# A pre-LN retention and mixture-of-experts layer on eight cores: smaller staging buffers, evacuation moved to VectorE, one copy of the odd heads, one wait ahead of the down projection

## The chip, the cores and the metric

One Trainium2 chip, all 8 of its cores. Each core takes one sequence of the batch (4096 tokens of 1024 features) and computes the whole layer for it; nothing is exchanged between cores. The metric is the device time of the slowest core, in microseconds (us), over one execution.

## The reference, cut to what matters

```python
x = x + attn(layernorm(x))      # retention: 16 heads of 64
x = x + ffn(layernorm(x))       # 8 experts and a shared one

# attn: Q, K, V = x @ Wq, Wk, Wv
scores = Q K^T * Dm / 8         # Dm: per head g**(i-j), lower triangle
out    = scores @ V             # no softmax
c      = groupnorm(out)         # one mean and variance per head over all 4096 tokens
return (c * gn_weight + gn_bias) @ Wout

# ffn: every expert on every token (g, u: 1024 -> 1408; w_down: 1408 -> 1024)
eo  = (silu(x @ w_gate[e]) * (x @ w_up[e])) @ w_down[e]
out = sum_e combine[e] * eo[e] + sigmoid(x @ shared_gate) * shared(x)
```

`combine` holds the renormalised softmax weights of the two best experts and zeros for the others, so all nine feed-forward blocks (eight experts and the shared one) run over all tokens.

## The kernel before, in words

Five instruction streams (TensorE, VectorE, ScalarE, SyncE, GpSimd) are written out by hand. `em(engine, fn)` appends to a stream and semaphores tie the streams together; each stream runs strictly in the order written. There are three blocks with a barrier of all engines between them.

**Block 0** (lines 212 to 242) loads the masks and the four attention matrices (cast to bf16 by the GpSimd queue's DMAs).

**Phase 1** (lines 312 to 622) runs over 8 chunks of 512 tokens. Per chunk, in order: ScalarE computes layer norm 1 (`emit_ln_sc`, line 123) from `x_sb`; TensorE transposes the result (`emit_t512a`); TensorE makes 24 groups of 8 matmuls, 8 each for q, k and v (`tqkv`, line 346), through two PSUM banks; each group is evacuated to bf16, q by VectorE (`vqkv`) and k and v by ScalarE (`sqkv`). The odd heads lie on partitions 64 to 127 and must be copied to partitions 0 to 63. SyncE does that in eight steps (`qk2`, line 402): for each `et` it waits for q and k of that `et`, issues one DMA of 64 KB from `qt_sb` and one from `kt_sb`, and waits until both have landed before the next step. Then come 16 steps of attention (`t_p1`, `v_1`, `s_ku`, `t_p2`, `v_2`, `s_tb`), of which the first, line 435 to 437, waits for all evacuations and all copies. At the end SyncE stores the chunk's output (`spill`), and VectorE and ScalarE gather the group norm's sums (`vstat`, `sstat`).

SyncE's order in a chunk is: load of the next chunk's x (`ldx`, after layer norm 1), wait for it, `qk2`, `spill`.

Alongside, GpSimd converts the expert weights to bf16: 27 pieces (nine blocks of gate, up, down), each 5.5 MB of f32 read from HBM into `stg` (2.75 MB as bf16) and then written back to `wbf`. One `stg` exists, so read and write alternate, each waiting for the one before to land (`emit_conversions`, line 284). Nothing ties these pieces to the chunks.

**Phase 2** (lines 777 to 1077) runs over 8 tiles of 512 tokens. Per tile: transposes with group norm folded in (`emit_t512b`), output projection (`twout`, line 835) and residual (`vwout`, line 848), layer norm 2, transposes, router, and then nine experts. For an expert TensorE makes 11 gate/up groups (16 matmuls each, lines 971 and 975). After each, ScalarE applies silu (line 987) and copies u (line 988), and VectorE multiplies them into `h_sb` (line 997). Then TensorE makes 8 down groups of 11 matmuls (`tdown`, line 1033), each evacuated by VectorE with a multiply-add into `x1` (line 1049). The first of the 8 groups (`didx == 0`) waits for the eleven blocks of h one at a time, just before the matmul that reads each:

```python
for it in range(NIT):
    if didx == 0:
        t.wait_ge(S("vch").h, htg[it])
    ins = t.matmul(db, ...)
```

The weights pass through `wring`, a ring of three slots of 2816 KB. The slots of gate and up come free together when ScalarE has copied the last u of the expert, so the loads for the next expert's gate and up (line 738, GpSimd's queue) start there and run beside the 88 down matmuls. The slot of down comes free after the last down group.

`x_sb` is one buffer of 4 x 1024 f32 per partition. In phase 2 the next tile's x is loaded into it after the output projection has read it (`ldx2`, line 860).

Of the kernel before, what the change touches and what calls it, by code (L numbers as in the profile page):

```python
# [10 lines left out]
F32 = mybir.dt.float32  # L11
# [6 lines left out]
C = 128  # L18
SC = 512
# [42 lines left out]
def build_nc(dbg=False, phases=(1, 2), nsc=None, p1_att=True, p1_qkv=True, p1_gn=True, p1_stats=True,  # L62
# [17 lines left out]
    dmask_h = nc.dram_tensor("dmask", [C, NH * C], F32, kind="ExternalInput").ap()  # L80
# [18 lines left out]
    x_sb = sb("x_sb", [C, 4 * D], F32)  # L99
    cols = sb("cols", [C, 32], F32)  # L100
    sqdump = sb("sqdump", [C, 2 * D], BF16)
# [3 lines left out]
    bcast = sb("bcast", [C, 32], F32)  # L105
# [17 lines left out]
    def emit_ln_sc(src, dst, per_tt_wait=None):  # L123
        ss = S("sc1")

        def s_ln(sc):
            for tt in range(4):
                if per_tt_wait is not None:
                    w = per_tt_wait[tt]
                    sc.wait_ge(S(w[0]).h, w[1])  # L130
                if tt >= 2:
                    sc.drain()
                sc.activation(sqdump[:, (tt % 2) * D:(tt % 2 + 1) * D],  # L133
                              src[:, tt * D:(tt + 1) * D], AF.Identity,
                              accum_out=cols[:, tt:tt + 1])
                sc.drain()
                sc.activation(sqdump[:, (tt % 2) * D:(tt % 2 + 1) * D],
                              src[:, tt * D:(tt + 1) * D], AF.Square,
                              accum_out=cols[:, 4 + tt:5 + tt])
# [33 lines left out]
    with contextlib.ExitStack() as p1es:  # L173
# [3 lines left out]
        dmask = sb1("dmask_sb", [C, NH * C], F32)  # L177
# [18 lines left out]
        stg = sb1("stg", [C, WSLOT], BF16)  # L196
# [87 lines left out]
        def emit_conversions(n):  # L284
            def gconv(g, plist=tuple(range(conv_state["p"], min(conv_state["p"] + n, PPT)))):
                for p in plist:
                    if p >= 1:
                        g.wait_ge(S("gcs0").h, 16 * p)
                    g.dma_start(out=stg[:, :], in_=conv_src(p)).then_inc(S("gcv0").h, 16)
                    g.wait_ge(S("gcv0").h, 16 * (p + 1))  # L290
                    g.dma_start(out=wbf_h[p], in_=stg[:, :]).then_inc(S("gcs0").h, 16)
            for p in range(conv_state["p"], min(conv_state["p"] + n, PPT)):
                S("gcv0").n += 16
                S("gcs0").n += 16
            conv_state["p"] = min(conv_state["p"] + n, PPT)
            em("gpsimd", gconv)
# [15 lines left out]
        for c in range(nsc):  # L312
# [30 lines left out]
            for gidx, (kind, idx) in enumerate(groups):  # L343
# [28 lines left out]
                if kind == "q":  # L372
                    def vqkv(v, idx=idx, bk=bk, tgt=S("peq").n):
                        v.wait_ge(S("peq").h, tgt)
                        ins = v.tensor_copy(qt_sb[:, idx * SC:(idx + 1) * SC], bk)
                        ins.then_inc(S("vcq").h, 1)
                    S("vcq").n += 1
                    evac_tgts.append(("vcq", S("vcq").n))
                    q_evac[idx] = ("vcq", S("vcq").n)
                    em("vector", vqkv)  # L380
                else:
                    def sqkv(sc, kind=kind, idx=idx, bk=bk, tgt=S("peq").n):
                        sc.wait_ge(S("peq").h, tgt)
                        if kind == "k":
                            dst = kt_sb[:, idx * SC:(idx + 1) * SC]
                        else:
                            tt, ec = idx // 2, idx % 2
                            dst = v_sb[:, tt * D + ec * 512:tt * D + (ec + 1) * 512]
                        ins = sc.copy(dst, bk)
                        ins.then_inc(S("scq").h, 1)  # L390
                    S("scq").n += 1
                    evac_tgts.append(("scq", S("scq").n))
                    if kind == "k":
                        k_evac[idx] = ("scq", S("scq").n)
                    em("scalar", sqkv)
            qkv_done_v = S("vcq").n
            qkv_done_s = S("scq").n

            for et in range(8):
                S("sld").n += 32  # L400
# [10 lines left out]
                em("sync", qk2)  # L411
# [11 lines left out]
            def emit_p1(m):  # L423
# [6 lines left out]
                def t_p1(t, ccx=ccx, heads=heads, a_bank=a_bank, ktr0=ktr0, m=m,  # L430
                         qtgt=qkv_done_v, stgt=qkv_done_s, q2tgt=qk2_done,
                         atgt=att_done_prev, vtgt=(vca_v1.get(m - 2, 0)),
                         kutgt=scku_m.get(m - 2, 0)):
                    if m < 2:
                        t.wait_ge(S("vcq").h, qtgt)
                        t.wait_ge(S("scq").h, stgt)
# [164 lines left out]
            def sstat(sc, tgt=att_done):  # L601
# [3 lines left out]
                for h in range(NH):  # L605
                    if h >= 2:
                        sc.drain()
                    ins = sc.activation(sqdump[:, (h % 2) * 256:(h % 2) * 256 + 256],
                                        src3[:, :, h * HE:(h + 1) * HE],
# [78 lines left out]
    with contextlib.ExitStack() as p2es:  # L688
# [87 lines left out]

        for t_i in range(NTILE):
            x1 = x1_sb[:, (t_i % 2) * 4 * D:(t_i % 2 + 1) * 4 * D]

            if t_i == 0:  # L780
                S("sld").n += 128

                def ld0(s, tgt=S("sld").n):
                    for tt in range(4):
                        s.dma_start(out=combt_sb[:, tt * D:(tt + 1) * D],
                                    in_=comb_h[tt * C:(tt + 1) * C, :]).then_inc(S("sld").h, 16)
                        ins = s.dma_start(out=x_sb[:, tt * D:(tt + 1) * D],
# [32 lines left out]
            for tloc in range(4):  # L820
                for dc in range(2):
# [21 lines left out]
                    def vwout(v, tloc=tloc, dc=dc, bk=bk, tgt=S("pew").n, x1=x1,  # L843
                              sttgt=(store_tgts[t_i - 2] if (gidx == 0 and t_i >= 2) else None)):
# [3 lines left out]
                        ins = v.tensor_add(x1[:, tloc * D + dc * 512:tloc * D + (dc + 1) * 512],  # L848
                                           x_sb[:, tloc * D + dc * 512:tloc * D + (dc + 1) * 512],
# [6 lines left out]

            if t_i + 1 < NTILE:
                S("sld").n += 64

                def ldx2(s, t_n=t_i + 1, wtgt=wout_done, tgt=S("sld").n):  # L860
                    s.wait_ge(S("vcw").h, wtgt)
                    for tt in range(4):
                        ins = s.dma_start(out=x_sb[:, tt * D:(tt + 1) * D],
# [88 lines left out]
            for e in range(NEXP):  # L952
                p0 = PPT * t_i + 3 * e
                hb = (e % 2) * NIT * SC
                h_tgts = {}
                for it in range(NIT):
# [45 lines left out]
                    h_tgts[it] = S("vch").n  # L1002
# [8 lines left out]
                for tloc in range(4):  # L1011
                    for dc in range(2):
# [4 lines left out]
                        def tdown(t, tloc=tloc, dc=dc, db=db, wd0=wd0, didx=didx, e=e,  # L1017
                                  htgt=h_done, ldd=piece_tgt[p0 + 2], hb=hb,
                                  htg=dict(h_tgts),
                                  banktgt=(S("vcd").n - 1 if (e > 0 or didx >= 2) else -1),  # L1020
                                  sctgt=router_sc_done):
# [61 lines left out]
def _make_consts():  # L1083
# [12 lines left out]
    return dmask, gcols, eye  # L1096
# [25 lines left out]
```

## Time and profile before

| | us |
|---|---|
| two timed executions | 5820.17 and 6282.54, median 6051.36 |
| the profiled execution | 5830.85 |
| its span on the slowest core (core 1), from first to last instruction | 5829.3 |
| spans of the eight cores | 5771.3 to 5829.3 |
| TensorE matmuls busy | 4933.5 (85%) |
| VectorE / ScalarE / GpSimd busy | 1348.8 / 1512.2 / 159.1 |
| phase 1 ends, phase 2 begins at about | 1243 |

The rows below come from the profiled execution, and all its times are counted from the first instruction on the core. The two timed executions lie 462 us apart; the profiled one stands within 11 us of the shorter. "Idle before" is the time that the engine stood still ahead of an instruction, and the arrow names what it then waited for.

### The profile page before, as it was taken

What the parts mean: (1) busy time and instruction counts of PE and PEld (TensorE: products, weight loads), DVE (VectorE), ACT (ScalarE), POOL (GpSimd) and SP (SyncE); (2) the same over time, 40 slices, a digit from 0 to 9 for tenths busy, and PEclk for the clock granted to TensorE, in tenths of its full rate; (3) what the DMA queues carried; (4) which work ended last, traced back from release to release, by engine and by line L of the source; (5) the groups of instructions that cost most, each with busy time, mean ns of one, the idle gap of its engine ahead of it and who ended that gap; (6) DMA issues with size and microseconds to landing.
All of it is one profiled execution on the core that took longest, in us unless ns stands there. A gap on an engine that the chain in (4) does not pass through costs nothing.

```text
span 5829.3 us, 66455 instructions; the slowest of 8 cores (5771.3 to 5829.3 us)
## 1 busy us (share of the span) xinstructions
PE 4933.5 (85%) x24644; PEld 2318.2 (40%) x24644; DVE 1348.8 (23%) x3473; ACT 1512.2 (26%) x3683; POOL 159.1 (3%) x279
## 2 busy tenths in 40 slices
PE   3544444648999899899989998999899989998999
PEld 1322222324444444444434443444344434443444
DVE  0333333332112211221121112111211121112111
ACT  1433444432212221221222122121312222122121
POOL 0000000000000000000000000000000000000000
PEclk9666666769999999999999999999999999999999
DMA  9888884033334334423343433334343342433433
GB/s 185 213 201 203 209 212 112 23 110 119 126 148 176 125 124 176 158 119 152 146 155 122 176 131 144 159 139 167 123 164 149 149 155 120 179 129 124 161 137 134
DMA packets 105895, 867.85 MB, mean 149 GB/s; under 512 B 10480, under 2 KB 18672, under 8 KB 74352
## 3 DMA queue, kind: packets, MB, share of 16 engines
q0 software_dynamic: 71728, 786.99, 39.8%
q1 hardware_dynamic: 33856, 76.62, 3.9%
q8 instruction: 206, 3.38, 0.2%
q14 instruction: 105, 0.86, 0.1%
HBM read 838.43 MB, written 103.02 MB: 162 GB/s over the span
## 4 chain that ended last, share of the span: by engine, by line
PE 61%; DMA 13%; ACT 2%; issue 1%; DVE 1%; POOL 0%; ACTq 0%; DVEq 0%; SPq 0%; POOLq 0%
PE psf L971 24%; PE psf L975 24%; DMA wring<-wbf 12%; PE psf L1033 10%; PE psf L835 2%; ACT xln_bf L164 1%; DMA x_sb<-x 1%; PE psb L756 1%; ACT silu_sb L987 0%; DVE combT L766 0%; POOL wring L738 0%; ACT ucp_sb L988 0%; DVE xln2T L770 0%; ACT L154 0%; ACT sqdump L133 0%
## 5 line engine op out<-in xcount | busy, mean ns | idle before, releaser
L971 PE MATMUL psf<-xln2T,wring 128*128 128x512 bf16 x6336 | 1518.2, 383 | 41.7 <-DMA wring<-wbf 41.4
L975 PE MATMUL psf<-xln2T,wring 128*128 128x512 bf16 x6336 | 1505.0, 381 | 0.0
L1033 PE MATMUL psf<-wring,h_sb 128*128 128x512 bf16 x6336 | 1379.6, 379 | 0.2
L987 ACT ACTIVATE silu_sb<-psf 128x512 bf16<-128x512 f32 x792 | 472.8, 597 | 3129.4 <-PE psf L975 3129.3
L971 PEld LDWEIGHTS psf<-xln2T,wring 128*128 128x128 bf16 x6336 | 620.3, 98 | 810.5 <-issue 84.7
L975 PEld LDWEIGHTS psf<-xln2T,wring 128*128 128x128 bf16 x6336 | 622.9, 98 | 757.1 <-issue 16.9
L1033 PEld LDWEIGHTS psf<-wring,h_sb 128*128 128x128 bf16 x6336 | 619.4, 98 | 748.7 <-issue 15.5
L997 DVE TENSOR_TENSOR h_sb<-silu_sb,ucp_sb 128x512 bf16<-128x512 bf16 x792 | 336.9, 425 | 2487.3 <-ACT ucp_sb L988 2487.3
L1049 DVE SCALAR_TENSOR_TENSOR x_sb<-psf,c_sb,x_sb 128x512 f32<-128x512 f32 x576 | 432.8, 751 | 870.1 <-PE psf L1033 870.1
L988 ACT CAST ucp_sb<-psf 128x512 bf16<-128x512 f32 x792 | 459.9, 581 | 0.0
L256 PE MATMUL psb<-eye_sb,xln_bf 128*128 128x128 bf16 x256 | 32.5, 302 | 316.2 <-ACT xln_bf L164 309.7
L738 POOL DMA_DIRECT2D wring<-wbf x216 | 113.5, 529 | 4720.5 <-ACT ucp_sb L988 3217.9
L446 PE MATMUL psf<-qt_sb,kt_sb 64*128 64x128 bf16 x512 | 75.7, 299 | 193.2 <-DMA kt_sb<-kt_sb 191.2
L508 DVE TENSOR_TENSOR am<-psf,dmask_sb 128x512 bf16<-128x512 f32 x128 | 86.3, 679 | 414.6 <-PE psb L450 414.6
L519 ACT ACTIVATE ku_sb<-psb,gcols_sb 128x64 bf16<-128x64 bf16 x512 | 118.8, 314 | 204.5 <-PE psb L450 194.7
L256 PEld LDWEIGHTS psb<-eye_sb,xln_bf 128*128 128x128 bf16 x256 | 22.9, 129 | 324.7 <-issue 322.8
L475 PE MATMUL psf<-v_sb,am 128*128 128x64 bf16 x512 | 47.4, 232 | 104.3 <-ACT ku_sb L519 101.7
L367 PE MATMUL psf<-xlnT,wq_bf 128*128 128x512 bf16 x512 | 126.3, 413 | 6.4 <-DVE xlnT L265 6.4
L756 PE MATMUL psb<-eye_sb,xln_bf 128*128 128x128 bf16 x256 | 32.4, 301 | 115.3 <-ACT xln_bf L164 109.3
L133 ACT ACTIVATE sqdump<-x_sb 128x1024 bf16<-128x1024 f32 x64 | 67.5, 1054 | 230.4 <-DVE x_sb L848 228.4
L835 PE MATMUL psf<-wout_bf,combT 128*128 128x512 bf16 x512 | 120.5, 399 | 7.9 <-DVE combT L766 7.9
L446 PEld LDWEIGHTS psf<-qt_sb,kt_sb 64*128 64x128 bf16 x512 | 43.1, 125 | 204.1 <-issue 196.9
(99 smaller groups left out, 1888.2 us busy)
## 6 DMA issues: line engine op xcount, KB each, us to landing
wring<-wbf POOLq DMA_DIRECT2D x216, 2816.0 KB, 10.8
wbf<-stg POOLq DMA_DIRECT2D x27, 2816.0 KB, 10.4
x_sb<-x SPq DMA_DIRECT2D x64, 512.0 KB, 6.9
stg<-wg POOLq DMA_DIRECT2D x8, 2816.0 KB, 19.7
stg<-wu POOLq DMA_DIRECT2D x8, 2816.0 KB, 19.4
stg<-wd POOLq DMA_DIRECT2D x8, 2816.0 KB, 19.9
out<-x_sb SPq DMA_DIRECT2D x32, 512.0 KB, 13.3
comb<-comb_sb SPq DMA_DIRECT2D x32, 256.0 KB, 3.8
```

The lines of the kernel that those rows point to most:

```text
L367: ins = t.matmul(bk, w, mv, start=(dt == 0), stop=(dt == 7))
L446: t.matmul(a_bank[:, hi * C:(hi + 1) * C], kt, qt, start=True, stop=True)
L519: ins = sc.mul(ku_sb[:, kur0 + hi * HE:kur0 + (hi + 1) * HE], psb[:, ktr0 + hi * HE:ktr0 + (hi + 1) * HE], gcols[:, NH + h:NH + h + 1])
L738: ins = g.dma_start(out=wring[:, (p % 3) * WSLOT:(p % 3) * WSLOT + WSLOT], in_=(wbf_h[p % PPT] if use_conv else conv_src2(p % PPT)))
L835: ins = t.matmul(bk, combT[:, dt * SC + tloc * C:dt * SC + (tloc + 1) * C], wout_bf[:, dt * D + dc * 512:dt * D + (dc + 1) * 512], start=( ...
L971: t.matmul(gb, wring[:, wg0 + dt * IFF + it * C:wg0 + dt * IFF + (it + 1) * C], xln2T[:, dt * SC:(dt + 1) * SC], start=(dt == 0), stop=(dt ...
L975: ins = t.matmul(ub, wring[:, wu0 + dt * IFF + it * C:wu0 + dt * IFF + (it + 1) * C], xln2T[:, dt * SC:(dt + 1) * SC], start=(dt == 0), st ...
L987: sc.activation(silu_sb[:, (it % 2) * SC:(it % 2 + 1) * SC], gb, AF.Silu)
L988: ins = sc.copy(ucp_sb[:, (it % 2) * SC:(it % 2 + 1) * SC], ub)
L997: ins = v.tensor_mul(h_sb[:, hb + it * SC:hb + (it + 1) * SC], silu_sb[:, (it % 2) * SC:(it % 2 + 1) * SC], ucp_sb[:, (it % 2) * SC:(it % ...
L1033: ins = t.matmul(db, h_sb[:, hb + it * SC + tloc * C:hb + it * SC + (tloc + 1) * C], wring[:, wd0 + it * D + dc * 512:wd0 + it * D + (dc + ...
L1049: ins = v.scalar_tensor_tensor(x1[:, tloc * D + dc * 512:tloc * D + (dc + 1) * 512], db, ccol, x1[:, tloc * D + dc * 512:tloc * D + (dc + ...
```

## The change

- `stg` shrinks from 11264 to 6144 columns, and each of the 27 conversion pieces is done in two halves (4 + 4 blocks of 128 rows for gate and up, 5 + 6 for down), still alternately read and written through the one buffer.
- All 24 groups of q, k and v are evacuated by VectorE; `sqkv` on ScalarE and the semaphore `scq` are gone.
- `qk2` is issued once per chunk, after all 24 evacuations, as two DMAs of 512 KB (rows of 8 KB on 64 partitions).
- `tdown` waits for all eleven blocks of h ahead of its first matmul.
- `x_sb` has two halves, and `ldx2` for tile t+1 waits for the output projection of tile t-1 in place of tile t.
- `sqdump` has one half, so ScalarE drains once more in each layer norm and in each `sstat`.
- `dmask` is bf16; `bcast` moves from the permanent buffers to those of phase 1.

```diff
@@ emit_conversions
-                    g.dma_start(out=stg[:, :], in_=conv_src(p)).then_inc(S("gcv0").h, 16)
-                    g.wait_ge(S("gcv0").h, 16 * (p + 1))
-                    g.dma_start(out=wbf_h[p], in_=stg[:, :]).then_inc(S("gcs0").h, 16)
+                    for hf in range(2):
+                        ph = 2 * p + hf
+                        if ph >= 1:
+                            g.wait_ge(S("gcs0").h, 16 * ph)
+                        g.dma_start(out=stg[:, 0:ncols],
+                                    in_=bass.AP(full.tensor, off, dims)).then_inc(S("gcv0").h, 16)
+                        g.wait_ge(S("gcv0").h, 16 * (ph + 1))
+                        g.dma_start(out=wbf_h[p][:, cols0:cols0 + ncols],
+                                    in_=stg[:, 0:ncols]).then_inc(S("gcs0").h, 16)
@@ qk2
-            for et in range(8):
-                def qk2(s, et=et, qw=q_evac[et], kw=k_evac[et], tgt=S("sld").n):
-                    s.wait_ge(S(qw[0]).h, qw[1])
-                    s.wait_ge(S(kw[0]).h, kw[1])
-                    s.dma_start(out=qt2_sb[:, et * SC:(et + 1) * SC],
-                                in_=qt_sb[HE:2 * HE, et * SC:(et + 1) * SC]).then_inc(S("sld").h, 16)
-                    ins = s.dma_start(out=kt2_sb[:, et * SC:(et + 1) * SC],
-                                      in_=kt_sb[HE:2 * HE, et * SC:(et + 1) * SC])
-                    ins.then_inc(S("sld").h, 16)
-                    s.wait_ge(S("sld").h, tgt)
+            def qk2(s, qtgt=qkv_done_v, tgt=S("sld").n):
+                s.wait_ge(S("vcq").h, qtgt)
+                s.dma_start(out=qt2_sb[:, :], in_=qt_sb[HE:2 * HE, :]).then_inc(S("sld").h, 16)
+                ins = s.dma_start(out=kt2_sb[:, :], in_=kt_sb[HE:2 * HE, :])
+                ins.then_inc(S("sld").h, 16)
+                s.wait_ge(S("sld").h, tgt)
@@ tdown
                             if didx == 0:
+                                t.wait_ge(S("vch").h, htgt)
                                 t.wait_ge(S(ldd[0]).h, ldd[1])
                                 if e == 0:
                                     t.wait_ge(S("scr").h, sctgt)
-                            elif didx == 1:
-                                t.wait_ge(S("vch").h, htgt)
                             if banktgt >= 1:
                                 t.wait_ge(S("vcd").h, banktgt)
                             for it in range(NIT):
-                                if didx == 0:
-                                    t.wait_ge(S("vch").h, htg[it])
@@ ldx2
-                def ldx2(s, t_n=t_i + 1, wtgt=wout_done, tgt=S("sld").n):
-                    s.wait_ge(S("vcw").h, wtgt)
+                def ldx2(s, t_n=t_i + 1, wtgt=wout_done_hist.get(t_i - 1, 0), tgt=S("sld").n):
+                    if wtgt:
+                        s.wait_ge(S("vcw").h, wtgt)
@@ emit_ln_sc (and sstat, h >= 1 in place of h >= 2)
-                if tt >= 2:
+                if tt >= 1:
                     sc.drain()
```

## Rows read from the trace of the kernel before

**Rows 1.** The page: DMA's busy share in 40 slices, in tenths

```profile
DMA  9888884033334334423343433334343342433433
```

**Rows 2.** Waits, core 1: engine, line waited for, us in total, times, longest

```profile
PE psf L446 <- DMA kt_sb<-kt_sb: 191.2, 6, 33.2
PE psf L971 <- DMA wring<-wbf: 41.4, 41, 3.9
POOL wring L738 <- POOLq L54: 312.0, 1, 312.0
```

**Rows 3.** Timeline, first chunk: start, us, engine, line, tile, count [idle before]

```profile
129.45 13.98 PE L367 MATMUL psf<-wv_bf,xlnT 128*128 128x512 bf16 x64
...
173.30 0.58 PE L446 MATMUL psf<-qt_sb,kt_sb 64*128 64x128 bf16 x4 [29.87 <-DMA kt_sb<-kt_sb]
```

**Rows 4.** DMA issues, whole span: count, KB each, median us to landing

```profile
dmask_sb<-dmask SPq DMA_DIRECT2D x1, 1024.0 KB, 5.1
```

**Rows 5.** Landing in phase 1: copies of kt (L407), spills (L585), x loads (L327)

```profile
DMA to landing us min/median/max: 2.0/5.2/10.2
...
DMA to landing us min/median/max: 2.2/3.8/13.2
...
DMA to landing us min/median/max: 5.5/8.8/18.1
```

**Rows 6.** Conversion: the reads' landing (L289), the writes' starts and landing (L291)

```profile
DMA to landing us min/median/max: 18.4/19.6/26.5
...
L291 POOL DMA_DIRECT2D wbf<-stg x27: 561/561/588, 88.9 to 931.0; - x27
...
DMA to landing us min/median/max: 9.4/10.4/14.5
```

**Rows 7.** Timeline, first expert: from the last up group into down

```profile
1365.43 1.89 PE L975 MATMUL psf<-xln2T,wring 128*128 128x512 bf16 x8
1367.16 19.16 PE L1033 MATMUL psf<-wring,h_sb 128*128 128x512 bf16 x88
...
1368.65 0.42 DVE L997 TENSOR_TENSOR h_sb<-silu_sb,ucp_sb 128x512 bf16<-128x512 bf16 x1 [3.03 <-ACT ucp_sb L988]
```

**Rows 8.** Timeline: VectorE's last piece and TensorE's start, behind one wait, then three

```profile
99.35 0.85 DVE L265 COPY xlnT<-psb 128x512 bf16<-128x512 bf16 x2 [0.41 <-PE psb L256]
100.35 1.01 PE L367 MATMUL psf<-xlnT,wq_bf 128*128 128x512 bf16 x2 [0.68 <-DVE xlnT L265]
...
1873.81 1.00 DVE L766 TENSOR_SCALAR combT<-psb,s 128x512 bf16<-128x512 bf16 x2 [0.19 <-PE psb L756]
1875.16 2.29 PE L835 MATMUL psf<-wout_bf,combT 128*128 128x512 bf16 x5 [1.01 <-DVE combT L766]
```

**Rows 9.** Timeline: TensorE at expert boundaries, core 1, last row core 6

```profile
1635.73 3.38 PE L971 MATMUL psf<-xln2T,wring 128*128 128x512 bf16 x8 [2.01 <-DMA wring<-wbf]
1638.90 2.13 PE L975 MATMUL psf<-xln2T,wring 128*128 128x512 bf16 x8
...
2208.86 1.89 PE L971 MATMUL psf<-xln2T,wring 128*128 128x512 bf16 x8 [1.88 <-DMA wring<-wbf]
...
1624.67 1.89 PE L971 MATMUL psf<-xln2T,wring 128*128 128x512 bf16 x8 [2.96 <-DMA wring<-wbf]
```

**Rows 10.** Windows: length, busy us of PE, PEld, DVE, ACT, POOL, granted clock, DMA

```profile
1636.00:1640.00 4.00, 4.00 (x12) 1.45 (x11) 0.00 (x0) 0.00 (x0) 0.00 (x0) 0.58 0.85 360
2209.00:2213.00 4.00, 4.00 (x20) 1.79 (x19) 0.00 (x0) 0.38 (x1) 0.00 (x0) 1.00 0.90 360
```

**Rows 11.** Timeline, layer norm 1: ScalarE without and with a drain ahead

```profile
78.48 0.19 ACT L137 ACTIVATION_READ_ACCUMULATOR sqdump<-x_sb 128x1 f32 x1
78.57 1.04 ACT L133 ACTIVATE sqdump<-x_sb 128x1024 bf16<-128x1024 f32 x1
79.52 0.19 ACT L133 ACTIVATION_READ_ACCUMULATOR sqdump<-x_sb 128x1 f32 x1
79.77 1.06 ACT L137 ACTIVATE sqdump<-x_sb 128x1024 bf16<-128x1024 f32 x1
```

More of the change, by code:

```diff
@@ L79, in build_nc @@
     swd_h = nc.dram_tensor("swd", [IFF, D], F32, kind="ExternalInput")
-    dmask_h = nc.dram_tensor("dmask", [C, NH * C], F32, kind="ExternalInput").ap()
+    dmask_h = nc.dram_tensor("dmask", [C, NH * C], BF16, kind="ExternalInput").ap()
     gcols_h = nc.dram_tensor("gcols", [C, 2 * NH], F32, kind="ExternalInput").ap()
@@ L175, in build_nc @@
         ps1 = lambda name, shape, dt: p1es.enter_context(nc.psum_tensor(name, shape, dt))
-        dmask = sb1("dmask_sb", [C, NH * C], F32)
+        dmask = sb1("dmask_sb", [C, NH * C], BF16)
         gcols = sb1("gcols_sb", [C, 2 * NH], F32)
@@ L195, in build_nc @@
         stattmp = sb1("stattmp", [C, 32], F32)
-        stg = sb1("stg", [C, WSLOT], BF16)
+        bcast = sb1("bcast", [C, 32], F32)
+        stg = sb1("stg", [C, 6 * D], BF16)
         psf = ps1("psf", [C, 6 * 512], F32)
@@ L286, in gconv @@
                 for p in plist:
-                    if p >= 1:
-                        g.wait_ge(S("gcs0").h, 16 * p)
-                    g.dma_start(out=stg[:, :], in_=conv_src(p)).then_inc(S("gcv0").h, 16)
-                    g.wait_ge(S("gcv0").h, 16 * (p + 1))
-                    g.dma_start(out=wbf_h[p], in_=stg[:, :]).then_inc(S("gcs0").h, 16)
+                    full = conv_src(p)
+                    if p % 3 != 2:
+                        halves = [(0, 4 * C * IFF, [[IFF, C], [C * IFF, 4], [1, IFF]], 4 * IFF),
+                                  (4 * IFF, 4 * C * IFF, [[IFF, C], [C * IFF, 4], [1, IFF]], 4 * IFF)]
+                    else:
+                        halves = [(0, 0, [[D, C], [C * D, 5], [1, D]], 5 * D),
+                                  (5 * D, 0, [[D, C], [C * D, 6], [1, D]], 6 * D)]
+                    for hf in range(2):
+                        ph = 2 * p + hf
+                        cols0, _, dims, ncols = halves[hf]
+                        off = full.offset + (hf * (4 * C * IFF) if p % 3 != 2 else hf * 5 * C * D)
+                        if ph >= 1:
[5 more added lines that the diff above has]
+                                    in_=stg[:, 0:ncols]).then_inc(S("gcs0").h, 16)
             for p in range(conv_state["p"], min(conv_state["p"] + n, PPT)):
-                S("gcv0").n += 16
-                S("gcs0").n += 16
+                S("gcv0").n += 32
+                S("gcs0").n += 32
             conv_state["p"] = min(conv_state["p"] + n, PPT)
@@ L370, in build_nc @@
                 em("tensor", tqkv)
[L372 to L395, printed above, removed]
@@ L396, in build_nc, with vqkv @@
[L396 to L411 removed]
+                def vqkv(v, kind=kind, idx=idx, bk=bk, tgt=S("peq").n):
+                    v.wait_ge(S("peq").h, tgt)
+                    if kind == "q":
+                        dst = qt_sb[:, idx * SC:(idx + 1) * SC]
+                    elif kind == "k":
+                        dst = kt_sb[:, idx * SC:(idx + 1) * SC]
+                    else:
+                        tt, ec = idx // 2, idx % 2
+                        dst = v_sb[:, tt * D + ec * 512:tt * D + (ec + 1) * 512]
+                    ins = v.tensor_copy(dst, bk)
+                    ins.then_inc(S("vcq").h, 1)
@@ new lines, in build_nc @@
+                S("vcq").n += 1
+                evac_tgts.append(("vcq", S("vcq").n))
+                em("vector", vqkv)
+            qkv_done_v = S("vcq").n
+            S("sld").n += 32
+            def qk2(s, qtgt=qkv_done_v, tgt=S("sld").n):
[4 more added lines that the diff above has]
+                s.wait_ge(S("sld").h, tgt)
@@ L412, in build_nc @@
+            em("sync", qk2)
             qk2_done = S("sld").n
@@ L786, in ld0 @@
                                     in_=comb_h[tt * C:(tt + 1) * C, :]).then_inc(S("sld").h, 16)
-                        ins = s.dma_start(out=x_sb[:, tt * D:(tt + 1) * D],
+                        ins = s.dma_start(out=xcur[:, tt * D:(tt + 1) * D],
                                           in_=x_h[tt * C:(tt + 1) * C, :])
@@ L1095, in _make_consts @@
     eye = np.eye(C, dtype=ml_dtypes.bfloat16)
-    return dmask, gcols, eye
+    return dmask.astype(ml_dtypes.bfloat16), gcols, eye
 def kernel(**inputs):
```

33 lines of the change are left out of this document (14 added, 19 removed).

## The prediction

> **What bounds the kernel now.** I first read the page's slices. DMA is busy at eight or nine tenths for about 940 us and then hardly at all until phase 2 [rows 1]: this is the conversion. GpSimd, whose queue it fills, issues its last write at 931.0 [rows 6] and then stands still for 312.0 us [rows 2], so the barrier is at about 1243. So phase 1 is bound by its chunks, not by the conversion, and in a chunk the chain goes through layer norm on ScalarE, 24 groups on TensorE, the copies of the odd heads, and attention. The waits name the copies as the one hole that the change touches: TensorE stands 191.2 us in six chunks ahead of the first attention matmul (L446) [rows 2]. In the first chunk the last of the 24 groups is over at about 143.4 and L446 starts at 173.3 [rows 3]. The copies of 64 KB take 5.2 us to land in the middle, 2.0 at best [rows 5], and eight rounds of them stand one behind the other. The two chunks behind the conversion's end do not wait.
>
> Phase 2 is bound by TensorE. Its only waits that matter here are for the weights of the next expert's gate and up, 41.4 us in 41 places [rows 2]. The down matmuls start 0.16 us before the last up group's modelled end, at 1367.16, while h of that group is ready only at 1368.65 + 0.42 = 1369.07 [rows 7]. Ten of the eleven matmuls of the first down group need earlier blocks, and the eleventh comes due about 2.2 us after the first. The wait by blocks therefore hides nearly the whole evacuation. The change removes that cover.
>
> **The change part by part.** The sum is made against the profiled execution, 5830.85 us. It lies near the shorter timed execution (5820.17) and 220 us under the median of the two (6051.36); nothing below explains the distance between those two.
>
> *Copies of the odd heads.* They can start after the last evacuation, now 0.9 us behind the last matmul; two issues take 1 us. For the landing of 1 MB in rows of 8 KB the nearest row is dmask, 5.1 us [rows 4]. So a chunk without the conversion waits about 7 us. Beside the conversion small copies take 5.2 instead of 2.0, at worst 10.2, spills 3.8 with 13.2 at worst, and x loads 8.8 with 18.1 at worst [rows 5]. I take 5 us more, 12 in all; the bounds are 7 and 20 (2 + 18.1). Seven chunks will be beside the conversion (see there) and one is not: 7 x 12 + 7 = 91 against 191.2, **-100 us**; bounds -135 (8 x 7) and -31 (8 x 20).
>
> *Evacuation by VectorE.* One group takes TensorE 13.98 / 8 = 1.75 us [rows 3]. VectorE already keeps up with it in the q groups, and in this stretch it has nothing else. This costs nothing while an evacuation takes less than 1.75. The bf16 mask leaves VectorE's multiply bound by the f32 scores that it reads, in my reading: zero. The earlier load of x in phase 2 is hidden on both sides, since only the first tile waits for x before: zero.
>
> *Drains.* ScalarE's next piece starts 0.09 us after the read of the accumulator begins without a drain and 0.25 us after it with one [rows 11]. That is 0.16 us in each of 16 layer norms and 8 `sstat`: **+4 us**.
>
> *Conversion in halves.* The starts of the 27 writes span 88.9 to 931.0, so a piece takes 842.1 / 26 = 32.4 us; landing of read and write (19.6 + 10.4) is most of it [rows 6]. Bytes stay, two DMAs are added. The cheapest landing in the trace is 2.0 us [rows 5]; with 0.6 for issue I take 2.6 each: 37.6 a piece, from 62 to 62 + 27 x 37.6 = 1077. Phase 1 would now end at 1243 - 96 = 1147, so this stays hidden with 70 us to spare, and only the eighth chunk's copies miss the conversion. With the middle landing of small copies, 5.2 + 0.6 each, a piece takes 44 us and the conversion ends at 1250: that is the other bound.
>
> *The wait ahead of the down matmuls.* It stands first of three waits (h, weights, bank or router). Behind one wait TensorE starts 0.15 us after VectorE's end (99.35 + 0.85 to 100.35); behind three, 0.35 us (1873.81 + 1.00 to 1875.16) [rows 8]. I take three, since the others are looked at only once h is there. The down matmuls then start at 1369.07 + 0.35 = 1369.42 in place of 1367.16: 2.26 us, 72 experts, **+163 us** (with 0.15: +148). What is queued behind it is the rest of the down matmuls, then the next expert, and nothing on other engines fills the hole. The loads for the next gate and up do not move, since their slots come free with the last copy of u. So the later down matmuls cover the present waits for them up to 2.1 us each: 41.4 us with the longest at 3.9, all but about 4, **-37 us**.
>
> *The clock.* The hole of 2.26 us between matmuls is 2.26 - 0.16 = 2.1 us as the rows count idle time. Behind an idle time of 2.01 us the granted clock was 0.58 of full speed in the mean over the next four microseconds, so mostly at the lower level of 1.2 GHz; behind 1.88 it stayed at 1.00, the upper level of 2.4 GHz [rows 9, 10]. At the lower level 16 matmuls took 3.38 + 2.13 where they otherwise take 1.89 + 1.89: 1.7 us lost. But an idle time of 2.96 on core 6 had no such effect (1.89 behind it) [rows 9], so not each hole is followed by it. Core 1 has six waits above 1.9 us, of which the row with 2.01 is the shortest, and all six were. Between these I take two of three: 48 x 1.7 = **+82 us**, with 0 and 72 x 1.7 = 122 as bounds, and the six of before (**-10 us**) go, as their waits are covered. The Trainium skill, page "TensorE: Matmul & The Clock Gate", section "HAM oscillation — how this bites in real kernels", has a rule of thumb that only idle gaps longer than any of these bring the clock down. By it this term would be nothing; the row behind 2.01 us speaks against it.
>
> Sum: -100 + 4 + 163 - 37 + 82 - 10 = +102, **5933 us** (+1.7%). The other cores lie 0 to 58 us lower now and have fewer waits to cover, so they draw up to core 1 and do not pass it by much.
>
> **The rivals.** *The clock holds.* The hole is at the edge between 1.88 and 2.01, so a start only 0.15 us behind h would bring it to 1.9. Then the 82 us go: 5851, about as before. For it speaks the row of core 6, against it the three waits in a row. It is also the case that the named rule of the skill leads to.
>
> *It falls at every hole.* 72 in place of 48: 5973. For it: all six of core 1.
>
> *The conversion becomes the bound (slower).* Its place is the barrier ahead of phase 2. It decides once a piece takes more than (1147 - 62) / 27 = 40.2 us, that is 3.9 us for each added DMA. At 44 us a piece all the gain of phase 1 is gone and 7 more: 5933 + 96 + 7 = 6036; halfway about 5985. Against it: the DMA queues are busy at eight to nine tenths now, so most of the time is bytes, which stay.
>
> *The one large copy is no quicker beside the conversion.* With 20 us each, the wait falls by 31 only: 5933 + 69 = 6002. For it: nothing is copied any longer under the k and v groups. Against it: spills of the same 1 MB.
>
> *The change of the wait costs nothing, because the weights bind anyway.* That would need waits of about 2 us at all 72 boundaries; there are 41 with 1 us in the mean. I give it no chance of its own.
>
> **How the numbers follow.** Forecast 0.45, clock holds 0.18, falls everywhere 0.15, conversion 0.10, large copy 0.12. The range goes from the first rival to the fourth, 5850 to 6005, and leaves out the far end of the conversion's case and the lucky corner of small copy waits with a held clock (5816). A measurement of this kernel tells about 2% from no change, 117 us: 5714 and 5947. No case reaches 5714; I leave 0.02. A fifth of the forecast's spread and all of three rivals lie above 5947: 0.10 + 0.15 + 0.10 + 0.12 = 0.47. The rest, 0.51, is no change.
>
> **What would show it.** The wait of L446 should fall from 191 to about 91 us, in eight chunks; phase 1 should end near 1147, with GpSimd still waiting for the barrier. A new wait of L1033 for VectorE's h should stand at 72 times, some 150 us. L971's wait for weights should fall under 10. The list of slices or windows at the starts of the down stretch should show a granted clock near 0.5 behind about two thirds of the holes, as 3.4 to 3.6 us for their first eight matmuls. A wait of GpSimd near zero at the barrier would make the conversion the bound and the forecast wrong; so would a chunk period above 145 us, or down matmuls that start less than 2 us late.

## The result, and the profile after

| | before | after |
|---|---|---|
| profiled execution, us | 5830.85 | 5948.68 |
| ratio of times, with its 95% interval | 1 | 1.0206 (1.0192 to 1.022) |
| median of all timed executions, us | 5827.03 (10) | 6297.69 (11) |
| spans of the eight cores, profiled | 5771.3 to 5829.3 | 5918.9 to 5947.1 |
| slowest core | 1 | 7 |
| TensorE matmuls busy on it | 4933.5 | 5031.8 |

The change made the kernel 2.1% slower. The ratio rests on executions between 5933.8 and 5946.3 us after and 5815.6 to 5830.0 before. In the other executions, of either kernel, the cores of one die or of both had a lower granted clock, and they are left out here and in all comparisons below.

The waits of core 7 after the change (engine, line waited for, us in total, times, longest):

```profile
PE psf L1025 <- DVE h_sb L994: 153.1, 72, 2.5
PE psf L441 <- DMA kt_sb<-kt_sb: 94.8, 8, 14.4
POOL wring L732 <- POOLq L54: 43.0, 1, 43.0
```

Line 441 is line 446 of before, 1025 is 1033 and 968 is 971. The wait for the copies of the odd heads is half of what it was on the core of [rows 2], and it now stands in all eight chunks. The wait of the down matmuls for h is new, once for each of the 72 experts. GpSimd's slack at the barrier shrank from 312.0 us [rows 2] to 43.0.

One chunk, same kernel and core (start, us, what, [idle before]):

```profile
147.22 0.53 SPq L403 DMA_DIRECT2D qt_sb<-qt_sb  x1
147.80 0.58 SPq L404 DMA_DIRECT2D kt_sb<-kt_sb  x1
160.72 0.58 PE L441 MATMUL psf<-qt_sb,kt_sb 64*128 64x128 bf16 x4 [14.37 <-DMA kt_sb<-kt_sb]
```

The two copies of 512 KB land 13 us after the issue of the second, and TensorE stands 14.37 us where it stood 29.87 [rows 3].

Now two expert boundaries of the same kernel, an earlier and a later one, and behind them the windows at the start of their down matmuls, the later one first (length, busy us of PE, PEld, DVE, ACT and POOL, granted clock, DMA):

```profile
1279.98 0.42 DVE L994 TENSOR_TENSOR h_sb<-silu_sb,ucp_sb 128x512 bf16<-128x512 bf16 x1 [3.03 <-ACT ucp_sb L985]
1280.77 3.40 PE L1025 MATMUL psf<-wring,h_sb 128*128 128x512 bf16 x15 [2.12 <-DVE h_sb L994]
...
1340.21 0.43 DVE L994 TENSOR_TENSOR h_sb<-silu_sb,ucp_sb 128x512 bf16<-128x512 bf16 x1 [3.03 <-ACT ucp_sb L985]
1341.00 4.22 PE L1025 MATMUL psf<-wring,h_sb 128*128 128x512 bf16 x11 [2.12 <-DVE h_sb L994]
```

```profile
1341.00:1345.00 4.00, 4.00 (x11) 1.46 (x12) 0.00 (x0) 0.00 (x0) 0.69 (x2) 0.58 0.53 180
1280.00:1284.00 4.00, 3.23 (x15) 1.50 (x16) 0.85 (x2) 0.00 (x0) 1.05 (x2) 1.00 0.31 90
```

Both holes are 2.12 us. Behind the first the clock stayed at the upper level (1.00, 2.4 GHz) and 15 matmuls took 3.40 us. Behind the second it was mostly at the lower one (0.58 in the mean, 1.2 GHz while it lasted) and 11 matmuls took 4.22. How often that happened is read from the busy time of the down matmuls on core 7, before (line 1033) and after (line 1025):

```profile
L1033 PE MATMUL psf<-wring,h_sb 128*128 128x512 bf16 x6336 | 1379.6, 379 | 0.2
```

```profile
L968 PE MATMUL psf<-xln2T,wring 128*128 128x512 bf16 x6336 | 1510.2, 381 | 3.6 <-DMA wring<-wbf 2.9 <-issue 0.5
L1025 PE MATMUL psf<-wring,h_sb 128*128 128x512 bf16 x6336 | 1464.8, 395 | 153.1 <-DVE h_sb L994 153.1
```

The same 6336 matmuls take 85.2 us more; at 1.7 us a fall that is 50 falls behind 72 holes.

### The profile page after: what moved, and what is told of

Same layout as the page of the kernel before. It is cut to its first block, busy times and chain, and to the rows that moved or that the text cites. A ratio compares the mean times of both kernels' runs of the same rounds, so it can differ in the third digit from the quotient of the medians.

```text
span 5947.1 us, 65490 instructions; the slowest of 8 cores (5918.9 to 5947.1 us)
## 1 busy us (share of the span) xinstructions
PE 5031.8 (85%) x24644; PEld 2341.5 (39%) x24644; DVE 1437.4 (24%) x3601; ACT 1439.4 (24%) x3555; POOL 190.0 (3%) x333
## 4 chain that ended last, share of the span: by engine, by line
PE 72%; ACT 3%; DMA 2%; DVE 1%; issue 1%; ACTq 0%; DVEq 0%; SPq 0%; POOL 0%; POOLq 0%
PE psf L968 23%; PE psf L972 23%; PE psf L1025 23%; PE psf L831 2%; DMA wring<-wbf 2%; ACT silu_sb L984 1%; ACT xln_bf L161 1%; PE psb L750 1%; DMA x_sb<-x 1%; ACT ucp_sb L985 1%; DVE h_sb L994 0%; DVE combT L760 0%; DVE xln2T L764 0%; ACT L151 0%; ACT sqdump L135 0%
## 5 line engine op out<-in xcount | busy, mean ns | idle before, releaser
L1025 PE MATMUL psf<-wring,h_sb 128*128 128x512 bf16 x6336 | 1464.8, 395 | 153.1 <-DVE h_sb L994 153.1
L1025 PEld LDWEIGHTS psf<-wring,h_sb 128*128 128x128 bf16 x6336 | 636.0, 101 | 981.8 <-issue 301.2
L441 PE MATMUL psf<-qt_sb,kt_sb 64*128 64x128 bf16 x512 | 77.2, 304 | 94.8 <-DMA kt_sb<-kt_sb 94.8
L556 ACT CAST tbf<-tf 64x64 bf16<-64x64 f32 x512 | 87.3, 240 | 131.0 <-DVE tf L543 131.0
L535 DVE SCALAR_TENSOR_TENSOR comb_sb<-psf,gcols_sb,oicp 128x64 bf16<-128x64 f32 x512 | 109.9, 277 | 10.9
```

The source lines that it names most:

```text
L535: v.scalar_tensor_tensor(comb_sb[:, ccx * D + h * HE:ccx * D + (h + 1) * HE], oio[:, 256 + hi * HE:256 + (hi + 1) * HE], gcols[:, h:h + 1] ...
L1025: ins = t.matmul(db, h_sb[:, hb + it * SC + tloc * C:hb + it * SC + (tloc + 1) * C], wring[:, wd0 + it * D + dc * 512:wd0 + it * D + (dc + ...
```

## The experiments

Every kernel was run beside the kernel before. Where a ratio is given it has its 95% interval; the other times rest on one or two executions each and are given as such, beside 5933.8 to 5946.3 for the changed kernel. The kernel before took 5827.3 to 5882.8 us beside the first four kernels below, and 5808.8 to 5822.4 beside the others. So the ratios of the first four come out some 0.6% lower than they would against the executions of the result, and their times in us are the surer comparison.

### The down wait alone, taken out and put in

**Wait by blocks again, in the changed kernel.**

```diff
                             if didx == 0:
-                                t.wait_ge(S("vch").h, htgt)
                                 t.wait_ge(S(ldd[0]).h, ldd[1])
@@
                             for it in range(NIT):
+                                if didx == 0:
+                                    t.wait_ge(S("vch").h, htg[it])
```

> The changed kernel with one part undone: the first down group waits for the eleven blocks of h one at a time again. Theory (the single wait opens a hole of 2.29 us at 72 places, 165 us, and the granted clock falls behind about 50 of them, 1.7 us each, 86 us; the holes cover the waits for weights, which come back): from about 5945 us down by 165 + 86 and up by 15 to 40, so 5715 to 5735 us, about 2% below the kernel before; no idle time of the down matmuls for h, waits for weights of 15 to 45 us. Rival (most of the loss in phase 2 is something else, the double x buffer or a later load): the time stays above 5830. Rival (the hole costs, the clock does not): about 5800 to 5815.

Measured: 5719.5 to 5726.1 us, ratio to the kernel before 0.9734 (0.9705 to 0.9762). Gate and down matmuls of its slowest core, lines 969 and 1031:

```profile
L969 PE MATMUL psf<-xln2T,wring 128*128 128x512 bf16 x6192 | 1499.3, 382 | 41.1 <-DMA wring<-wbf 30.2 <-issue 3.4
...
L1031 PE MATMUL psf<-wring,h_sb 128*128 128x512 bf16 x6208 | 1372.9, 379 | 6.9
```

The down matmuls no longer wait, their mean is back at 379 ns, and waits for weights of 30.2 us have come back. (The counts differ from 6336 since some records are missing from this trace.) The time lies in the range that was expected. This one part of the change costs about 220 us, more than the whole change lost. (Against the 5815.6 to 5830.0 us of the result this kernel is 1.7% faster than the kernel before.)

**The single wait, in the kernel before.** The reverse edit.

```diff
                             if didx == 0:
+                                t.wait_ge(S("vch").h, htgt)
                                 t.wait_ge(S(ldd[0]).h, ldd[1])
@@
-                                if didx == 0:
-                                    t.wait_ge(S("vch").h, htg[it])
```

> The kernel before with this one part of the change alone: one wait for all eleven blocks of h ahead of the first down matmul. Theory: +165 (holes) +86 (clock) -16 to -49 (waits for weights covered, by core), slowest core 6030 to 6050 us against about 5827. Rival (the clock falls only together with the rest of the change): about 5960. Phase 1 unchanged, the wait of the first attention matmul near 190 us.

Measured: 6033.5 to 6043.7 us, ratio 1.027 (1.024 to 1.03). Waits, then matmuls, of its slowest core:

```profile
PE psf L446 <- DMA kt_sb<-kt_sb: 182.2, 6, 32.6
PE psf L1030 <- DVE h_sb L997: 153.1, 72, 2.5
```

```profile
L971 PE MATMUL psf<-xln2T,wring 128*128 128x512 bf16 x6336 | 1511.4, 382 | 20.6 <-DMA wring<-wbf 20.0 <-issue 0.2
L1030 PE MATMUL psf<-wring,h_sb 128*128 128x512 bf16 x6336 | 1442.9, 391 | 153.1 <-DVE h_sb L997 153.1
```

The hole is the same 153.1 us at 72 places, so it does not depend on the rest of the change, and the time came out where the holes and the clock together put it, not at the rival's 5960. On this core 63 us of clock are lost (1442.9 against 1379.6) and 20 us of waits for weights remain, so the two terms shift between cores while the sum stays near 6035. At 1.7 us a fall this core had about 37 falls behind the same 72 holes, where core 7 of the changed kernel had 50: the share of falls is no constant of the hole. (Against the executions of the result the ratio would be 1.037.)

### The hole and the clock, taken apart

**The wait for h last.** Same wait, same place, but behind the two others.

```diff
                             if didx == 0:
-                                t.wait_ge(S("vch").h, htgt)
                                 t.wait_ge(S(ldd[0]).h, ldd[1])
@@
                             if banktgt >= 1:
                                 t.wait_ge(S("vcd").h, banktgt)
+                            if didx == 0:
+                                t.wait_ge(S("vch").h, htgt)
```

> The changed kernel with the wait for h put behind the two other waits (weights, bank) in place of ahead of them; nothing else. Theory of the prediction (each further wait that stands behind the one that ends last delays the start by 0.1 us, so three waits give 0.35 us behind VectorE's end and one gives 0.15): the down matmuls start 2.06 in place of 2.27 us late, 72 x 0.21 = 15 us less. What the clock does separates two cases: a hole of 2.06 us lies between 2.05 (clock held) and 2.16 (clock fell) of the trace before. If the clock holds, 50 falls of 1.7 us go as well: 5945 - 15 - 86 = about 5845 us. If it falls as often as before: about 5930. Rival (the waits are not taken one after the other): no change, 5945.

Measured: 5844.3 and 5845.4 us. One boundary, then the group of all down matmuls, on its slowest core:

```profile
1336.23 0.42 DVE L994 TENSOR_TENSOR h_sb<-silu_sb,ucp_sb 128x512 bf16<-128x512 bf16 x1 [3.03 <-ACT ucp_sb L985]
...
1336.80 3.40 PE L1026 MATMUL psf<-wring,h_sb 128*128 128x512 bf16 x15 [1.90 <-DVE h_sb L994]
```

```profile
L1026 PE MATMUL psf<-wring,h_sb 128*128 128x512 bf16 x6336 | 1379.1, 379 | 137.5 <-DVE h_sb L994 137.5
```

TensorE now starts 0.15 us behind VectorE's end (1336.65 to 1336.80) in place of 0.37 (1280.40 to 1280.77). The waits fall from 153.1 to 137.5 us, 0.22 us at each place, as two waits less behind the last one should give. And the clock holds: the down matmuls are back at 1379.1 us, and on no core do they lose more than 3.4 us, two falls. In these two kernels a hole of 1.90 us leaves the clock alone and one of 2.12 brings it down at two of three places. Moving one line is worth about 100 us, of which 16 are the start and 85 the clock.

**The same, with the hole filled.** Eight matmuls whose result is thrown away stand ahead of the wait.

```diff
+                            if didx == 0:
+                                for dt in range(8):
+                                    t.matmul(db, xln2T[:, dt * SC:dt * SC + C],
+                                             xln2T[:, dt * SC:(dt + 1) * SC],
+                                             start=(dt == 0), stop=(dt == 7))
+                                t.wait_ge(S("vch").h, htgt)
```

> The changed kernel with the wait for h last, as in the run before, and eight matmuls of 512 columns ahead of it whose result is thrown away (they go into the bank that the first down group then clears), so that TensorE works through 1.7 of the 2.06 us that it would stand; the output is unchanged. Theory: the true work starts just as late, 72 x 2.06 = 148 us, but the granted clock does not fall behind the expert's last up group at all: about 5845 us, with short falls of the clock only at the tile boundaries. Rival (the clock's falls are not caused by the hole): no gain, 5930 to 5945. Rival (the extra matmuls delay the true ones): above 5845 by 72 x the delay, at 0.3 us each 5867.

Measured: 5838.7 and 5841.2 us, ratio 0.9963 (0.9842 to 1.0084). True and filling matmuls:

```profile
L1030 PE MATMUL psf<-wring,h_sb 128*128 128x512 bf16 x6336 | 1379.0, 379 | 13.3 <-DVE h_sb L994 13.3
L1025 PE MATMUL psf<-xln2T 128*128 128x512 bf16 x576 | 136.1, 379 | 0.0
```

TensorE hardly stands any more (13.3 us), the true work starts just as late, and the time is that of the run before within 7 us. The rival of delayed true matmuls (5867) falls. What is left of the loss is the late start by itself, whether TensorE stands or works through it: about 118 us against the wait by blocks in the changed kernel (5719.5 to 5726.1), which is 148 us of lateness less 30 of waits for weights. The clock had held in the run before already, without the extra matmuls. So this run shows that they cost no time, and not that they keep the clock up; filling the hole of 2.12 us was not tried. That the 85 us in the changed kernel are the clock's answer to the length of the hole rests on the run before.

### The copies of the odd heads

**Eight steps again, in the changed kernel.** `qk2` as before the change, with all evacuations on VectorE.

```diff
-            def qk2(s, qtgt=qkv_done_v, tgt=S("sld").n):
-                s.wait_ge(S("vcq").h, qtgt)
-                s.dma_start(out=qt2_sb[:, :], in_=qt_sb[HE:2 * HE, :])...
+            for et in range(8):
+                def qk2(s, et=et, qw=q_evac[et], kw=k_evac[et], tgt=S("sld").n):
+                    (as before the change)
```

> The changed kernel with the copies of the odd heads in eight steps again, each waiting for its two small copies to land; VectorE still evacuates everything and the conversion stays in halves. Theory (the gain of phase 1 is the copies' latency, paid once in place of eight times a chunk): TensorE's wait ahead of the first attention matmul goes from 95 back to at least 190 us, to about 240 if all chunks now lie beside the longer conversion; the time rises from about 5945 to 6040 to 6090 us. Rival (the gain came from VectorE's evacuation, which lets the attention start at once): no change, 5945.

Measured: 6002.9 us (one execution, the profiled one). Its waits:

```profile
PE psf L449 <- DMA kt_sb<-kt_sb: 151.9, 7, 26.1
...
POOL wring L740 <- POOLq L54: 140.0, 1, 140.0
```

The direction is right and the rival falls, but the wait came back to 151.9 and not to 190 or more, and the time to 6002.9 and not to 6040 or more. The time follows the wait: +57.1 us of wait, and +58 us against the median of the changed kernel's timed executions, 5944.9. On the eight cores the wait is 136.6 to 153.6 us, where the changed kernel has 80.9 to 95.7.

**One step, in the kernel before.** Nothing else is changed: ScalarE evacuates k and v, and the pieces are whole.

```diff
+                s.wait_ge(S("vcq").h, qtgt)
+                s.wait_ge(S("scq").h, stgt)
+                s.dma_start(out=qt2_sb[:, :], in_=qt_sb[HE:2 * HE, :])...
+                ins = s.dma_start(out=kt2_sb[:, :], in_=kt_sb[HE:2 * HE, :])
```

> The kernel before with the copies of the odd heads merged into two DMAs per chunk behind all evacuations; k and v are still evacuated by ScalarE, the conversion is in whole pieces, the wait for h is by blocks. Theory: the wait of the first attention matmul goes from about 190 to 75 to 90 us, the rest stays, so 5827 - 105 = about 5720 us. If VectorE's evacuation or the halves had a cost of their own in phase 1, this kernel's phase 1 would end before 1154 - 10 us; if they had a gain, after 1165. Rival (one large copy needs the halved conversion to get through between its parts): waits of 20 us per chunk, about 5790 us.

Measured: 5730.1 and 5739.6 us, ratio 0.9862 (0.9837 to 0.9888).

```profile
POOL wring L735 <- POOLq L54: 182.5, 1, 182.5
PE psf L443 <- DMA kt_sb<-kt_sb: 104.8, 8, 14.5
```

The merged copies alone are worth 80 to 90 us, and the rival of 20 us a chunk (5790) falls. The wait is 104.8 where 75 to 90 was expected, 98.8 in the mean of the eight cores, against 89.4 in the changed kernel; the cores of one run lie up to 20 us apart in it, so the difference between the kernels is uncertain. The first loads of phase 2 leave at 1160.0 on this core, between the 1144 and 1165 named above, so neither a cost nor a gain of VectorE's evacuation or of the halves shows here.

**Eight steps, one wait for landing, in the kernel before.** SyncE issues each pair as soon as its q and k are there.

```diff
-                    s.wait_ge(S("sld").h, tgt)
+                    if et == 7:
+                        s.wait_ge(S("sld").h, tgt)
```

> The kernel before with the eight steps of copies, but SyncE waits for their landing only once, after the eighth, so that each pair is issued as soon as its q and k are there and their latencies overlap with each other and with the v groups. Theory (what costs is the latency paid in series, not the bytes): the wait of the first attention matmul falls from about 190 to under 20 us, and the time from 5827 to 5640 to 5660 us; the conversion then still ends (at about 945) well ahead of phase 1 (at about 1060). Rival (the copies' total time beside the conversion is what costs): a wait of 60 us or more, no better than 5710 us.

Measured: 5644.1 to 5674.1 us, ratio 0.9724 (0.9692 to 0.9755). SyncE's last pairs of one chunk, and the last v groups on ScalarE:

```profile
254.33 0.46 SPq L405 DMA_DIRECT2D qt_sb<-qt_sb  x1
254.84 0.58 SPq L407 DMA_DIRECT2D kt_sb<-kt_sb  x1
256.06 0.46 SPq L405 DMA_DIRECT2D qt_sb<-qt_sb  x1
256.56 0.58 SPq L407 DMA_DIRECT2D kt_sb<-kt_sb  x1
```

```profile
265.76 0.59 ACT L389 CAST v_sb<-psf 128x512 bf16<-128x512 f32 x1 [1.14 <-PE psf L367]
267.49 0.59 ACT L389 CAST v_sb<-psf 128x512 bf16<-128x512 f32 x1 [1.14 <-PE psf L367]
```

A pair leaves every 1.7 us in place of every 7, and the last one at 256.6 has 11 us of v groups ahead of it to land under; one such copy takes 6.8 us in the middle here. No wait for these copies is left in the trace. What cost 191 us was eight latencies in a row, not bytes. This is the fastest kernel of the study: three of its four executions took 5644.1 to 5650.3 us.

### The conversion in halves, and the second x buffer

**Whole pieces and one x buffer, in the changed kernel.**

```diff
-        stg = sb1("stg", [C, 6 * D], BF16)
+        stg = sb1("stg", [C, WSLOT], BF16)
-    x_sb = sb("x_sb", [C, 2 * 4 * D], F32)
+    x_sb = sb("x_sb", [C, 4 * D], F32)
-                def ldx2(s, t_n=t_i + 1, wtgt=wout_done_hist.get(t_i - 1, 0), tgt=S("sld").n):
+                def ldx2(s, t_n=t_i + 1, wtgt=wout_done, tgt=S("sld").n):
```

> The changed kernel with the conversion in whole pieces again and the single x_sb (the memory of its second half goes to stg), ldx2 waiting for the same tile's output projection. Theory (both parts cost and bring nothing while the conversion ends ahead of the chunks): 5945 us, at most 15 less since the last chunk's copies miss the conversion; GpSimd's wait at the barrier grows from 43 to about 210 us. Rival (the second x buffer brings something in phase 2): above 5960. Rival (the halves slow the chunks by contention): below 5920.

Measured: 5955.0 and 5956.9 us.

```profile
POOL wring L719 <- POOLq L54: 182.6, 1, 182.6
PE psf L428 <- DMA kt_sb<-kt_sb: 102.4, 8, 14.4
```

About 15 us slower than the changed kernel and not faster, against my expectation, though within neither rival. 11 us of it is the wait for the copies: 100.4 us in the mean of the eight cores (91.7 to 102.4) against 89.4 (80.9 to 95.7). The rest isn't resolved by two executions. The second x buffer has no part in it that the traces show: with one buffer and with two, TensorE waits for x in phase 2 only once, ahead of the first tile.

**Halves alone, in the kernel before.** The conversion of the changed kernel, nothing else.

> The kernel before with the conversion in halves alone. It asks why the wait for the small copies came back to 152 us only, and not to 190, in the changed kernel with eight steps. If the halves do it (shorter bursts of the conversion between the copies): the wait of the first attention matmul is 140 to 170 us in place of about 190 although up to eight chunks now lie beside the conversion, and the time is 5827 - 20 to 50, about 5790 us. If VectorE's evacuation of k and v does it (the k copies can start no earlier, so this would be odd): wait 190 us or more, 240 with all chunks beside the conversion, time 5830 to 5880 us. The conversion itself ends at 1060 to 1110 in place of 941.

Measured: 5787.0 us in the profiled execution and 5857.1 in another; the kernel before took 5812.1 to 5816.3 beside it.

```profile
PE psf L459 <- DMA kt_sb<-kt_sb: 167.2, 7, 26.0
POOL wring L751 <- POOLq L54: 136.1, 1, 136.1
```

The wait for small copies is 167.2 us, on the side of the halves, with ScalarE still evacuating. So a chunk's small copies get through sooner beside the halved conversion, 23.9 us a chunk (167.2 / 7) against 31.9 (191.2 / 6). It is so on every core: 141.0 to 167.2 us in seven chunks, where the kernel before has 174.0 to 194.2 in six. The middle landing of one copy of kt hardly moved (5.0 to 5.6 us by core, 5.2 to 5.7 before), but the longest fell to 7.8 to 8.9 from 10.0 to 12.2. The profiled execution is 25 to 29 us shorter than the kernel before, about what the wait lost; the other does not show it, so the gain of the whole kernel is less certain than that of the wait.

### Both orders mended, in the changed kernel

Wait by blocks and eight steps of copies with one wait for landing, with halves, VectorE's evacuation and both x buffers kept.

> The changed kernel (halves, VectorE's evacuation, two x buffers) with both costly orders mended: the wait for h by blocks, and the copies in eight steps with a single wait for landing. Theory (with the wait for copies gone, neither the halves nor the evacuating engine matter): 5640 to 5660 us, like the kernel before with the same copies (5649). If the conversion in halves now becomes the bound (phase 1 would end at about 1065, the conversion at about 1080 to 1110): GpSimd's wait at the barrier is zero and the time 5670 to 5700 us.

Measured: 5656.7 to 5666.2 us, ratio 0.9736 (0.9714 to 0.9758). GpSimd's wait at the barrier:

```profile
POOL wring L741 <- POOLq L54: 7.4, 1, 7.4
```

Two of its three executions lie in the expected range and one 6 us above. It is some 10 us behind most executions of the kernel before with the same copies (5644.1 to 5650.3, one at 5674.1), so the other parts of the change together cost little once the copies no longer wait. But with 7.4 us the halved conversion is about to become the bound.

## Why the prediction was right or wrong

I forecast 5933 us and a change inside 2%; the profiled execution took 5948.68 and the ratio is 1.0206. The mechanisms and nearly all sizes held. By term, in the trace:

| term | predicted | core 1 | core 7 |
|---|---|---|---|
| phase 1, up to the first gate matmul | -96 | 1326.3 to 1233.1: -93.2 | 1316.1 to 1238.5: -77.6 |
| holes ahead of the down matmuls | +163 | +165 | +165 |
| waits for weights covered | -37 | -48 | -11 |
| clock behind the holes | +82 | +81.8 | +85.2 |
| falls of before that go, and the rest | -10 | -4 | +4 |
| sum | +102 | +101 | +165 |

(Holes: 153.1 as listed and 0.16 at each of 72 places; the waits for weights count the same 0.16. The last row but one is what the busy times of the other matmuls moved.)

*The step that failed* is the sentence that the other cores draw up to core 1 and do not pass it by much. Core 1 took 101 us more, as summed, and was no longer the slowest. (That its sum fits within 1 us is luck in part: its misses of +3 in phase 1, +2 in the holes, -11 in the waits for weights and +6 in the falls of before cancel.) The terms -37 and -10 were read on core 1, which was the slowest before mostly because it waited longest for weights (41.4 us). On core 7 those waits were 10.7 us (its own row of before), so there was little for the holes to cover:

```profile
L971 PE MATMUL psf<-xln2T,wring 128*128 128x512 bf16 x6336 | 1510.1, 381 | 11.5 <-DMA wring<-wbf 10.7 <-issue 0.3
```

The rows of core 1 after the change, where nothing is left of its waits for weights:

```profile
L968 PE MATMUL psf<-xln2T,wring 128*128 128x512 bf16 x6336 | 1510.1, 381 | 0.3 <-DMA wring<-wbf 0.2
L1025 PE MATMUL psf<-wring,h_sb 128*128 128x512 bf16 x6336 | 1461.4, 395 | 153.1 <-DVE h_sb L994 153.1
```

Core 7 went from 5782.3 to 5947.1 and ended 16.6 us behind core 1. Those 16.6 us are made of small things: its phase 2 begins 5.4 us later, 3.8 us of waits for weights are left on it, and the clock costs it 3.4 us more in the down matmuls and 4 us more in the others. The first term is the mis-sized one. The copies saved this core 86 us (181.1 to 94.8) and not 100, since it had waited less for them than core 1, and 9 us of the rest of phase 1 went the other way where I had counted 4. By its own waits the terms give 5782.3 - 86 + 4 + 163 - 11 + 82, about 5934. So the sums made on core 1 and on core 7 both end 13 to 16 us short of the slowest core, and that was the distance to the 2% mark, which I had put at 5947 and given a chance of 0.47. Nothing singles out core 7: in the profiled and the five compared executions of the changed kernel the slowest core was 7, 0, 2, 0, 4 and 7.

*The copies* were sized right in what they leave: 91 us forecast and 94.8 measured (80.9 to 95.7 over the cores), 12 us a chunk beside the conversion against 11.9 in the mean and 14.4 at most. The 5 us that the conversion adds were a choice between bounds. But all eight chunks lay beside the conversion, since a piece takes (1111.6 - 81.3) / 53 x 2 = 38.9 us and not 37.6. These are the writes of the halves:

```profile
L301 POOL DMA_DIRECT2D wbf<-stg x54: 549/549/579, 81.3 to 1111.6; - x54
```

*The wait behind three waits* (0.35 us) and *the share of falls* (two of three) held, 50 of 72; the run with the wait last shows that the first makes the second. The share was chosen between bounds and not read from a row, so it is luck in part: the same hole in the kernel before gave core 0 about 37 falls. That run also is the rival "the clock holds", forecast at 5851 and measured at 5844 to 5845 once the start came 0.15 us behind h. The rule of thumb of the Trainium skill, page "TensorE: Matmul & The Clock Gate", section "HAM oscillation — how this bites in real kernels", that only longer idle gaps than these bring the clock down, does not hold in this kernel: gaps of 2.12 us did at 50 of 72 places.

*Conversion as the bound* did not come about: 43.0 us of slack were left (20.8 on the core with the least) where 70 were forecast. In the mended kernel it is 7.4.

*The halves* I costed at nothing beside their own length. They shorten the wait for small copies from 31.9 to 23.9 us a chunk and, less surely, for large ones from 100.4 to 89.4 over a run, in the mean of the cores. Why is open: each DMA of the conversion moves half the bytes and there are twice as many of them with a wait between, but no run separated the two. *VectorE's evacuation* cost nothing that a run shows, and the bf16 mask nothing either, as the multiply of the scores before and after shows:

```profile
L508 DVE TENSOR_TENSOR am<-psf,dmask_sb 128x512 bf16<-128x512 f32 x128 | 86.3, 679 | 414.6 <-PE psb L450 414.6
```

```profile
L503 DVE TENSOR_TENSOR am<-psf,dmask_sb 128x512 bf16<-128x512 f32 x128 | 86.1, 677 | 96.1 <-PE psb L445 96.1
```

## What to carry to other kernels

Where an engine waits for several semaphores ahead of its work, put the one that is fulfilled last at the end, or wait for each block just before the instruction that reads it: here the one was worth 100 us and the other 220. When small transfers are issued in a loop, don't wait for each to land; issue as their data comes and wait once. And look at each core, since what a new stall covers differs between them (10.7 to 41.4 us of waits here).

## What the runs showed of the hardware that I had not expected

The clock's answer is sharp: at 72 places a hole of 1.90 us left the down matmuls at 1379.1 us (at most 3.4 us more on other cores), and one of 2.12 us at the same places made them 1464.8. And work that is thrown away had no price in time there: with eight such matmuls ahead of the wait the kernel took 5838.7 and 5841.2 us, and 5844.3 and 5845.4 without them.
